# Attention scores from two fp32r parts of q and k in half of the array's rows, in a new order of TensorE's work

## The chip, the cores and the metric

The kernel runs on one core of one Trainium2 chip. The metric is the device time of one execution, in microseconds (us); the kernel before takes 1211.42 us, the median of three runs (1211.42, 1213.09, 1211.42).

## The reference, cut to what matters

One layer of a vision transformer on 8 images of 512 tokens of 256 features. Only the first part is touched, self-attention with 16 heads of 16 features:

```python
qkv = jnp.einsum('bysd,ed->byse', x, w_qkv) + b_qkv
qkv = qkv.reshape(B, S, NUM_HEADS, 3 * HEAD_DIM).transpose(0, 2, 1, 3)
q, k, v = jnp.split(qkv, 3, axis=-1)
logits = jnp.einsum('bhqd,bhkd->bhqk', q, k) / math.sqrt(HEAD_DIM)
attn = jax.nn.softmax(logits, axis=-1)
vals = jnp.einsum('bhqk,bhkd->bhqd', attn, v)
```

After it come the output projection, a state-space layer, and a feed-forward layer with one shared expert and two of eight routed ones. The change leaves them as they are.

## The kernel before

The kernel has four parts: the projections to q, k and v (up to about 108 us of the span), the attention (108 to about 504 us), and then the state-space and shared layers and the routed experts, which fill the rest.

**Projections** (`stage_qkv`). For each of the 8 images ("batch" in the code) TensorE makes four tiles of q and k (`project`, L309, in fp32) and four of v (L318). A score of q and k needs more precision than one bf16 product gives, so each value is cut into three bf16 parts: ScalarE rounds to the high part (L355), VectorE subtracts it (L400), ScalarE rounds the rest to the middle part (L360), VectorE subtracts again (L405). The parts go to DRAM, and are loaded back as rows for the scores. Behind the products of the later images TensorE scores the first two units ahead ("pairs", L286) into `fold_ps`, and VectorE reads their maxima (L413).

**Attention** (`attention_programs`). The work is cut in 32 units: image b times group g of four heads. One unit has 16 tiles by key and 16 tiles by query, 128x512 each. A tile by query (`score_by_query`, L653) serves only to find the maximum of each query's row: VectorE reads two such tiles at once (`take_max`, L746). It is made two units ahead. A tile by key (`score_by_key`, L662) has the keys on the partitions and has the maxima subtracted already, since these stand as more rows of the product; ScalarE takes its exponential straight out of PSUM (L806). The product with the values (`add_pv`, L673) uses the four column strips of the array for the four heads of a group, in fp32. For a product the six pairings of parts stand one under the other, 6 x 16 = 96 rows (99 with the three parts of the maximum).

The way of a maximum: VectorE's result is split in parts by GpSimd (`split_max`, L128 to L135), turned by TensorE (`turn_max`, L685) into a bank of `by_key`, copied out by ScalarE (L799), and put by a DMA from GpSimd's queue into the rows of q (`place_max`, L140). The next unit's first tile by key waits for that (`max_in`).

**What sets the order.** It is written out by hand. Each engine runs its own list, and semaphores join them. In `tensor.unit` the loop over j = 0 to 15 issues tile j by key, then as many tiles by query as `QUERIES[j % 4]` says, and at some j the products with the values (`LATE_PV`, `EARLY_PV`), the turn of the maxima (`MAX_BEHIND`) and the turn of the finished heads (`TURN_HEADS`). The tiles by key go round three banks of PSUM (`KEY_BANKS = 3`): a tile, or a turn of maxima, waits until ScalarE has read what was put three jobs earlier (`key_bank_free`). The tiles by query have four banks, two pairs. The last two units have no tiles by query; there `beside` puts work of the next stage between the tiles by key.

## Time and profile before

| | |
|---|---|
| median of three runs | 1211.42 us |
| the profiled execution | 1215.23 us, its span 1213.4 us |
| TensorE busy | 1156.5 us, 95% |
| VectorE busy | 785.6 us, 65% |
| ScalarE busy | 504.9 us, 42% |
| granted TensorE clock, mean | 0.988 |

### The profile page before, as it was taken

The numbers are of one execution on the slowest core, as the hardware profiler recorded it, in microseconds if no ns is written. First come the engines' busy times: TensorE is split into PE (matmuls) and PEld (weight loads), VectorE is DVE, ScalarE is ACT, GpSimd is POOL, SyncE is SP. The second block draws the span as 40 slices with busy tenths as digits, with TensorE's granted clock in tenths as the row PEclk, the third lists the DMA queues.
The fourth block names the chain that finished last, engine by engine and source line by source line (L and its number), as shares of the span: only waits on it lengthen the run. The fifth ranks groups of instructions, "written<-read, shape, count | busy, mean of one in ns | idle before, by whom it ended". The sixth has DMA issues, their size and how long they took to land.

```text
span 1213.4 us, 20444 instructions
## 1 busy us (share of the span) xinstructions
PE 1156.5 (95%) x5606; PEld 693.2 (57%) x5607; DVE 785.6 (65%) x1404; ACT 504.9 (42%) x890; POOL 395.7 (33%) x515
## 2 busy tenths in 40 slices
PE   6998999999999999989999999987999999999996
PEld 3654333333333334556655666556888888888885
DVE  3688888888888887687887677774333333333332
ACT  3444777777777777522122121421222221222221
POOL 3002621010101010223334433263554445554443
PEclk9998999999999999999999999998999999999999
DMA  8885333232323332124225541222333333333332
GB/s 304 254 263 173 88 86 88 84 105 68 103 71 100 88 84 63 55 103 105 48 57 105 104 87 40 66 36 53 50 48 51 52 53 52 50 49 50 51 53 35
DMA packets 108685, 105.32 MB, mean 87 GB/s; under 512 B 42464, under 2 KB 97904, under 8 KB 108624
## 3 DMA queue, kind: packets, MB, share of 16 engines
q1 hardware_dynamic: 90528, 81.18, 24.2%
q0 software_dynamic: 18112, 23.57, 11.4%
q8 instruction: 24, 0.39, 0.1%
q14 instruction: 21, 0.17, 0.1%
HBM read 64.88 MB, written 39.68 MB: 86 GB/s over the span
## 4 chain that ended last, share of the span: by engine, by line
PE 64%; issue 15%; POOL 5%; DVE 4%; DMA 2%; ACT 1%; SPq 0%; POOLq 0%; DVEq 0%; ACTq 0%
PE mix_pairs L73 17%; PE pv L673 10%; PE mix_made L1730 10%; PE by_key L662 10%; PE by_query L653 8%; PE mix_turn L1723 3%; PE mix_made L1198 2%; DVE k_mix_u L1404 2%; POOL mix_h L1067 2%; POOL mix_h L1064 1%; PE mix_turn L1703 1%; POOL kept_table L1083 1%; PE by_query L694 1%; POOL mix_rstd L1054 1%; DVE mix_stats L1394 1%
## 5 line engine op out<-in xcount | busy, mean ns | idle before, releaser
L746 DVE TENSOR_REDUCE k_neg_max<-by_query 128x2 f32<-128x1024 f32 x240 | 282.6, 1219 | 55.8 <-PE by_query L653 55.1
L806 ACT ACTIVATE k_wu_e<-by_key 128x512 f32<-128x512 f32 x512 | 278.4, 600 | 84.9 <-PE by_key L662 81.5
L662 PE MATMUL by_key<-k_wg_e 99*128 99x512 bf16 x512 | 180.4, 385 | 3.1 <-DVE pv L782 3.0
L1682 POOL DMA_INDIRECT out_rows<-x_y,k_slot x72 | 114.0, 1583 | 178.2 <-DVE x_y L1811 160.5
L1772 ACT ACTIVATE x_gate<-mix_pairs 128x512 f32<-128x512 f32 x72 | 43.0, 597 | 305.9 <-PE mix_pairs L73 305.9
L653 PE MATMUL by_query<-k_wg_e 96*128 96x512 bf16 x480 | 145.1, 383 | 0.3
L1730 PE MATMUL mix_made<-k_wd_e,x_acts_T 128*128 x576 | 136.0, 379 | 0.8 <-ACT x_acts_T L1781 0.8
L673 PE MATMUL pv<-k_wu_e,k_wd_e 128*17 128x512 f32 x1024 | 134.5, 598 | 0.2 <-ACT k_wu_e L806 0.2
L73 PE MATMUL mix_pairs<-w_short,x_T 128*128 x288 | 134.2, 466 | 0.0
L662 PEld LDWEIGHTS by_key<-k_wg_e 99*128 99x128 bf16 x512 | 42.4, 97 | 144.3 <-ACT k_wu_e L806 81.0
L1730 PEld LDWEIGHTS mix_made<-k_wd_e,x_acts_T 128*128 128x128 f32 x576 | 108.8, 189 | 18.8 <-issue 1.0
L73 PE MATMUL mix_pairs<-w_short,x_rest 128*128 x288 | 114.0, 396 | 0.0
L1795 DVE CAST x_T<-mix_turn 128x256 fp32r<-128x256 f32 x72 | 30.6, 424 | 106.2 <-PE mix_turn L1703 104.7
L128 POOL CAST k_max_parts<-k_neg_max 128x16 bf16<-128x16 f32 x32 | 6.4, 201 | 251.7 <-PE by_key L662 231.0
L1811 DVE TENSOR_SCALAR x_y<-mix_made,k_slot 128x256 f32<-128x256 f32 x72 | 34.8, 483 | 78.0 <-DMA out_rows<-x_y,k_slot 56.7
L915 POOL DMA_INDIRECT k_x_in<-kept_x_rows,k_slot x72 | 72.9, 1013 | 27.2 <-issue 21.6
L653 PEld LDWEIGHTS by_query<-k_wg_e 96*128 96x128 bf16 x480 | 45.0, 99 | 61.4 <-DVE k_wd_e L760 13.3
L1804 DVE TENSOR_TENSOR x_acts<-x_gate,mix_pairs 128x512 f32<-128x512 f32 x72 | 49.5, 687 | 46.4 <-PE mix_pairs L73 46.4
L1083 POOL DMA_INDIRECT kept_table<-k_pay,k_slot_i x64 | 64.6, 1009 | 22.3 <-issue 18.4
L309 PE MATMUL qk_ps<-k_wu_e,k_wqkv 128*128 128x512 f32 x128 | 60.1, 612 | 9.5 <-DMA k_wu_e<-in_xT 9.5
L1241 PE MATMUL mix_pairs<-k_mix_u_T,k_wg_s 128*128 128x512 f32 x128 | 64.4, 627 | 4.5 <-DVE mix_act_T L1376 4.5
L73 PEld LDWEIGHTS mix_pairs<-w_short,x_rest 128*128 128x128 f32 x288 | 54.5, 189 | 13.5
(220 smaller groups left out, 1722.6 us busy)
## 6 DMA issues: line engine op xcount, KB each, us to landing
k_wg_e<-kept_qk SPq DMA_DIRECT2D x384, 64.0 KB, 2.1
kept_qk<-k_qk_parts SPq DMA_DIRECT2D x32, 384.0 KB, 2.9
kept_v<-k_v_ones SPq DMA_DIRECT2D x8, 544.0 KB, 5.1
k_wd_e<-kept_v SPq DMA_DIRECT2D x32, 136.0 KB, 2.6
k_wu_e<-in_xT POOLq DMA_DIRECT2D x8, 512.0 KB, 5.8
kept_heads<-k_wd_e SPq DMA_DIRECT2D x8, 512.0 KB, 2.9
k_heads_in<-kept_heads SPq DMA_DIRECT2D x8, 512.0 KB
k_wg_e<-in_wg_e SPq DMA_DIRECT2D x8, 512.0 KB, 4.6
```

The lines of the kernel that those rows point to most:

```text
L73: mm = pe.matmul(out, short(lhs[a]), short(rhs[b]), start=(start and n == 0), stop=(stop and n == 2))
L309: mm = pe.matmul(qk_ps[:, j, :], wqkv[:, c, j * P:(j + 1) * P], xt[:, par, c, :], start=(c == 0), stop=(c == DC - 1))
L653: pe.matmul(by_query[:, pair_bank(b, g, k // 2) + k % 2, :], q_rows[0:KROWS, g, h, t * P:(t + 1) * P], k_rows[0:KROWS, g, h, :], start=Tru ...
L662: pe.matmul(by_key[:, key_bank(job), :], k_rows[0:SROWS, g, h, kt * P:(kt + 1) * P], q_rows[0:SROWS, g, h, :], start=True, stop=True).then ...
L673: mm = pe.matmul(pv[PV_ROWS * h:PV_ROWS * h + VW, :], v_unit[:, g, kt, h, :], probs[:, G * (kt // 2) + h, kt % 2, :], start=(kt == 0), sto ...
L746: dve.tensor_reduce(neg_max[:, g % 2, 2 * n:2 * n + 2], by_query[:, bank:bank + 2, :], AX.X, ALU.max, negate=True).then_inc(query_read, 1)
L806: act.activation(probs[:, key_tile(j) // 2 * G + j // 2 % G, j % 2, :], by_key[:, key_bank(job), :], ACT.Exp, scale=float(HD) ** -0.5).the ...
L915: pool.indirect_dma_start(out=mem["x_in"][:, r % FIRST_X, :], out_offset=None, in_=dram["x_rows"], in_offset=bass.IndirectOffsetOnAxis(ap= ...
L1083: pool.indirect_dma_start(out=dram["table"], in_offset=None, in_=mem["pay"][:, 1 - par, t, n, :], out_offset=bass.IndirectOffsetOnAxis(ap= ...
L1241: mm = pe.matmul(pairs[:, m % 2, n, :], w[:, c, m * P:(m + 1) * P], u2_T[:, c, :], start=(c == 0), stop=(c == DC - 1))
L1682: pool.indirect_dma_start(out=dram["out"], in_=y[:, r % 2, :], in_offset=None, compute_op=ALU.add, out_offset=bass.IndirectOffsetOnAxis(ap ...
L1730: mm = pe.matmul(ps_y[:, r % 2, 0:D], acts_T[:, m, :], mem["wd_e"][:, bass.ds(e, 1), m, :], start=(m == 0), stop=(m == FC - 1))
```

## The change

q and k are cut in two parts instead of three, in fp32r (fp32 data that TensorE multiplies in one pass), so there are three pairings, 3 x 16 = 48 rows, and 50 with the maximum's two parts. These fit half of the partitions. `rows_of(g)` puts groups 0 and 3 into partitions 0 to 63, and 1 and 2 into 64 to 127; the tiles by key of unit g and those by query of unit g + 2 thus always lie in different halves. The tiles in the projections pair group 0 with group 1. ScalarE's middle part and VectorE's low part go away. The parts in DRAM hold 8 bytes a value instead of 6; a unit is loaded by 6 DMAs of twice the size instead of 12. In the projections the scores ahead move into the last four images, and the turn of the first maxima to the end of the last image; the loads of the first units move from images 1, 3, 5, 6 to 1, 2, 5, 6. In a unit, the order of TensorE's work, the place of the turns and of ScalarE's copies change.

```diff
-PARTS = 3
-Q_PART = (0, 0, 0, 1, 1, 2)
-K_PART = (0, 1, 2, 0, 1, 0)
+PARTS = 2
+Q_PART = (0, 0, 1)
+K_PART = (0, 1, 0)
...
-MAX_BEHIND = 3
-HEADS_BEHIND = 5
+MAX_BEHIND = 8
+HEADS_BEHIND = 4
...
+def rows_of(g, count=HALF, first=0):
+    half = HALF * ((g + 1) // 2 % 2)
+    return slice(half + first, half + count)
...
     pool.sem_inc(step)
-    pool.tensor_copy(mem["max_parts"][:, 0, :], rows).then_inc(done, 1)
+    pool.tensor_copy(short(mem["max_parts"][:, 0, :]), rows).then_inc(done, 1)
     pool.wait_ge(done, base + 1)
-    pool.tensor_tensor(mem["neg_rest"][:, :], rows, mem["max_parts"][:, 0, :], ALU.subtract).then_inc(done, 1)
-    pool.wait_ge(done, base + 2)
-    pool.sem_inc(step)
-    pool.tensor_copy(mem["max_parts"][:, 1, :], mem["neg_rest"][:, :]).then_inc(done, 1)
-    pool.wait_ge(done, base + 3)
-    pool.tensor_tensor(mem["max_parts"][:, 2, :], mem["neg_rest"][:, :], mem["max_parts"][:, 1, :],
-                       ALU.subtract).then_inc(done, 1)
+    pool.tensor_tensor(short(mem["max_parts"][:, 1, :]), rows, mem["max_parts"][:, 0, :], ALU.subtract).then_inc(done, 1)
...
-        PAIR_BATCH = B - 5
-        TURN_BATCH, TURN_BEHIND = B - 2, 1
+        PAIR_BATCH = B - 4
+        PAIR_BEHIND = {b: (("qk", 0), ("qk", 2), ("v", 0), ("v", 2)) for b in range(PAIR_BATCH, B - 1)}
...
+                h, t = pair // TT, pair % TT
+                for g in range(2):
+                    rows = rows_of(g, KROWS)
+                    mm = pe.matmul(fold_ps[:, g, :], short(q_rows[rows, 0, h, t * P:(t + 1) * P]),
+                                   short(k_rows[rows, 0, h, :]), start=True, stop=True)
...
+                if isinstance(b, int) and b == B - 1:
+                    turn_first_max()
...
-            def middle_part(b, j):
-                act.wait_ge(qk_out[j], b + 1)
-                act.activation(qk_parts[:, j, 1, :], qk_rest[:, j, :], ACT.Copy).then_inc(middle_made, 1)
...
-            def low_part(b, j):
-                dve.wait_ge(middle_made, 4 * b + j + 1)
-                dve.tensor_tensor(qk_parts[:, j, 2, :], qk_rest[:, j, :], qk_parts[:, j, 1, :],
-                                  ALU.subtract).then_inc(cut[j], 1)
...
-    LATE_PV = {3: 2, 7: 3}
-    EARLY_PV = {11: 0, 15: 1}
-
-    QUERIES = (0, 2, 2, 0)
-    TURN_HEADS = 12
+    LATE_PV = {2: 2, 6: 3}
+    EARLY_PV = {10: 0, 14: 1}
+
+    QUERIES = (1, 1, 0, 2)
+    TURN_HEADS = 10
+
+    COPY_PV = 8
...
             pe.matmul(by_query[:, pair_bank(b, g, k // 2) + k % 2, :],
-                      q_rows[0:KROWS, g, h, t * P:(t + 1) * P], k_rows[0:KROWS, g, h, :],
+                      short(q_rows[rows_of(g, KROWS), g // 2, h, t * P:(t + 1) * P]), short(k_rows[rows_of(g, KROWS), g // 2, h, :]),
...
-            pe.matmul(by_key[:, key_bank(job), :], k_rows[0:SROWS, g, h, kt * P:(kt + 1) * P],
-                      q_rows[0:SROWS, g, h, :], start=True, stop=True).then_inc(key_filled, 1)
+            pe.matmul(by_key[:, key_bank(job), :], short(k_rows[rows_of(g, SROWS), g // 2, h, kt * P:(kt + 1) * P]),
+                      short(q_rows[rows_of(g, SROWS), g // 2, h, :]), start=True, stop=True).then_inc(key_filled, 1)
...
             for j in range(G * TT):
                 score_by_key(b, g, j)
+                if j == MAX_BEHIND and next_max:
+                    turn_max(b1, g1)
+                if j == TURN_HEADS and prev:
+                    turn_heads(bp, gp)
                 for _ in range(QUERIES[j % 4]):
...
-                if j == 7 and not (isinstance(b, int) and b == 0 and g == 0):
+                if j == COPY_PV and not (isinstance(b, int) and b == 0 and g == 0):
```

TensorE in the middle of a unit before, from a product with the values (`pv`) to the next; the rows L661 are register work of the sequencer:

```order
L673 MATMUL pv<-k_wu_e,k_wd_e 17x512 x4
L661 REGISTER_ALU
L662 MATMUL by_key<-k_wg_e 128x512
L661 REGISTER_ALU
L662 MATMUL by_key<-k_wg_e 128x512
L653 MATMUL by_query<-k_wg_e 128x512 x2
L661 REGISTER_ALU
L662 MATMUL by_key<-k_wg_e 128x512
L652 REGISTER_ALU
L653 MATMUL by_query<-k_wg_e 128x512 x2
L661 REGISTER_ALU
L662 MATMUL by_key<-k_wg_e 128x512
```

There were four tiles by key and four by query between two products with the values, the tiles by query two by two. The same place in the changed kernel (`by_key` is now L643, `by_query` L634, `pv` L654):

```order
L654 MATMUL pv<-k_wu_e,k_wd_e 17x512 x4
L642 REGISTER_ALU
L643 MATMUL by_key<-q_rows,k_rows 128x512
L633 REGISTER_ALU
L634 MATMUL by_query<-k_rows,q_rows 128x512 x2
L642 REGISTER_ALU
L643 MATMUL by_key<-q_rows,k_rows 128x512
L634 MATMUL by_query<-k_rows,q_rows 128x512
L642 REGISTER_ALU
L643 MATMUL by_key<-q_rows,k_rows 128x512
L634 MATMUL by_query<-k_rows,q_rows 128x512
L642 REGISTER_ALU
```

A fourth tile by key ends the piece, and the next product with the values stands right behind it: still four and four, but they alternate, and the fourth tile by key is the last thing before the values. The one piece of a unit that holds both turns, in the changed kernel, right behind tile 8 by key (L666 turns the maxima, L675 the heads):

```order
L666 MATMUL by_key<-k_ident,k_wd_e 128x128
L633 REGISTER_ALU
L634 MATMUL by_query<-k_rows,q_rows 128x512
L642 REGISTER_ALU
L643 MATMUL by_key<-q_rows,k_rows 128x512
L634 MATMUL by_query<-k_rows,q_rows 128x512
L642 REGISTER_ALU
L643 MATMUL by_key<-q_rows,k_rows 128x512
L672 REGISTER_ALU
L675 MATMUL by_query<-k_ident,heads_T 128x128 x4
L654 MATMUL pv<-k_wu_e,k_wd_e 17x512 x4
```

Before, the turn of the maxima (L685) stood behind tile 3 and the turn of the heads (L694) behind tile 12. ScalarE's list at the same place (L787 is the exponential, L780 the copy of the turned maxima, L799 that of the finished heads out of `pv`):

```order
L787 ACTIVATE k_wu_e<-by_key 128x512
L777 REGISTER_ALU
L780 ACTIVATE k_wd_e<-by_key 32x128
L797 REGISTER_ALU
L798 REGISTER_ALU
L799 ACTIVATE heads_T<-pv 128x512
L786 REGISTER_ALU
```

Both copies now stand behind exponential 8; before, they stood behind exponentials 3 and 7.

## Rows read from the trace of the kernel before

**Rows 1.** Busy time, 60 us of attention: span, PE, PEld, DVE, ACT, POOL, clock, DMA.

```profile
240.00:300.00 60.00, 59.53 (x343) 18.54 (x341) 49.24 (x51) 46.23 (x90) 7.23 (x25) 1.00 0.31 87
```

**Rows 2.** Turns of the maxima, one a unit: ns min/median/max, first and last start.

```profile
L685 PE MATMUL by_key<-k_identb,k_max_parts x31: 219/227/314, 110.5 to 476.1; 128*128 128x128 bf16 x31
```

**Rows 3.** Timeline of TensorE in one unit: start, duration, engine, line, count.

```profile
302.43 0.38 PE L662 MATMUL by_key<-k_wg_e 99*128 99x512 bf16 x1
302.75 1.05 PE L673 MATMUL pv<-k_wu_e,k_wd_e 128*17 128x512 f32 x8
303.73 0.60 PE L662 MATMUL by_key<-k_wg_e 99*128 99x512 bf16 x2
304.17 0.60 PE L653 MATMUL by_query<-k_wg_e 96*128 96x512 bf16 x2
...
305.87 1.05 PE L673 MATMUL pv<-k_wu_e,k_wd_e 128*17 128x512 f32 x8
...
308.69 1.05 PE L673 MATMUL pv<-k_wu_e,k_wd_e 128*17 128x512 f32 x8
```

**Rows 4.** Timeline, the turn of the heads in a unit.

```profile
300.58 0.60 PE L694 MATMUL by_query<-k_ident,heads_T 128*128 128x128 f32 x4
301.02 0.38 PE L662 MATMUL by_key<-k_wg_e 99*128 99x512 bf16 x1
```

**Rows 5.** Timeline of TensorE in the projections, and where the attention begins.

```profile
48.08 0.60 PE L286 MATMUL fold_ps<-k_wg_e 96*128 96x512 bf16 x2
48.51 3.60 PE L309 MATMUL qk_ps<-k_wu_e,k_wqkv 128*128 128x512 f32 x8
...
103.31 1.89 PE L318 MATMUL v_ps<-k_wqkv,k_wu_e 128*128 128x256 f32 x8
108.17 0.61 PE L662 MATMUL by_key<-k_wg_e 99*128 99x512 bf16 x2 [2.97 <-DVE pv L782]
```

**Rows 6.** Timeline of the experts: fp32r matmuls and their weight loads (PEld).

```profile
1000.99 0.19 PEld L73 LDWEIGHTS mix_pairs<-w_short,x_T 128*128 128x128 f32 x1
1001.02 0.48 PE L73 MATMUL mix_pairs<-w_short,x_T 128*128 x1
1001.10 0.19 PEld L73 LDWEIGHTS mix_pairs<-wu_rest,x_T 128*128 128x128 f32 x1
1001.33 0.40 PE L73 MATMUL mix_pairs<-wu_rest,x_T 128*128 x1
```

**Rows 7.** Groups by line, whole span: busy, mean ns of one, idle before.

```profile
L662 PEld LDWEIGHTS by_key<-k_wg_e 99*128 99x128 bf16 x512 | 42.4, 97 | 144.3 <-ACT k_wu_e L806 81.0 <-ACT k_max_rows L799 25.5 <-issue 8.1
L405 DVE TENSOR_TENSOR k_qk_parts<-k_wu_e,k_qk_parts 128x512 bf16<-128x512 f32 x32 | 21.8, 682 | 0.3
```

**Rows 8.** Timeline of VectorE: two readings of maxima; normalising between two.

```profile
121.95 2.36 DVE L746 TENSOR_REDUCE k_neg_max<-by_query 128x2 f32<-128x1024 f32 x2 [0.47 <-PE by_query L653]
...
301.22 0.26 DVE L756 RECIPROCAL row_sum<-by_query 128x16 f32<-128x16 f32 x1 [0.26 <-PE by_query L694]
...
301.87 1.22 DVE L746 TENSOR_REDUCE k_neg_max<-by_query 128x2 f32<-128x1024 f32 x1
```

**Rows 9.** Timeline, ScalarE and GpSimd behind the tiles by key.

```profile
304.16 1.57 ACT L806 ACTIVATE k_wu_e<-by_key 128x512 f32<-128x512 f32 x3 [0.71 <-PE by_key L662]
306.17 0.26 ACT L799 ACTIVATE k_max_rows<-by_key 48x128 bf16<-48x128 bf16 x1
307.12 0.62 POOL L140 DMA_DIRECT2D k_wg_e<-k_max_rows  x1 [1.54 <-ACT k_max_rows L799]
```

**Rows 10.** Timelines of the first unit: TensorE waits there for a bank.

```profile
110.70 0.60 ACT L806 ACTIVATE k_wu_e<-by_key 128x512 f32<-128x512 f32 x1 [0.53 <-PE by_key L662]
...
111.35 0.61 PE L662 MATMUL by_key<-k_wg_e 99*128 99x512 bf16 x1 [0.16 <-ACT k_wu_e L806]
```

**Rows 11.** DMA issues of the page: count, size each, median us to landing.

```profile
kept_qk<-k_qk_parts SPq DMA_DIRECT2D x32, 384.0 KB, 2.9
```

**Rows 12.** Line L140: the DMA of the maxima, all 32.

```profile
DMA to landing us min/median/max: 2.1/2.7/5.1
```

More of the change, by code:

```diff
@@ L166, in stage_qkv @@
         x_used = [sem(f"x_used{n}") for n in range(2)]
-        qk_out = [sem(f"qk_out{n}") for n in range(4)]
         cut = [sem(f"cut{n}") for n in range(4)]
@@ L220, in _ @@
             pool.wait_ge(ones_set, 2)
-            pool.memset(mem["k_rows"][KROWS:SROWS, :, :, :], 1.0).then_inc(ones_set, 1)
+            for half in range(2):
+                pool.memset(mem["k_rows"][HALF * half + HALF // 2:HALF * (half + 1), :, :, :], 1.0).then_inc(ones_set, 1)
             with pool.Fori(1, B // 2) as i:
@@ L256, in store @@
                         sp.wait_ge(parts_stored[j], 16)
-                        for n in range(ROW_LOADS // 4 * j, ROW_LOADS // 4 * (j + 1)):
+                        for n in LOAD_BEHIND[j]:
                             load_rows(sp, mem, dram, 0, unit, n)
@@ L266, in _ @@
             store(0)
+            sp.wait_ge(ones_set, 4)
             for b in range(1, B):
@@ L281, in score_pair @@
                     pe.wait_ge(pair_read, pair)
-                if pair == FIRST_PAIR[TURN_BATCH]:
-                    pe.wait_ge(first_copied, 1)
-                for k in (2 * n, 2 * n + 1):
-                    h, t = k // TT, k % TT
-                    mm = pe.matmul(fold_ps[:, k % 2, :], q_rows[0:KROWS, g, h, t * P:(t + 1) * P],
-                                   k_rows[0:KROWS, g, h, :], start=True, stop=True)
+                h, t = pair // TT, pair % TT
+                for g in range(2):
+                    rows = rows_of(g, KROWS)
+                    mm = pe.matmul(fold_ps[:, g, :], short(q_rows[rows, 0, h, t * P:(t + 1) * P]),
+                                   short(k_rows[rows, 0, h, :]), start=True, stop=True)
                 mm.then_inc(pair_scored, 1)
@@ L417, in cut_and_add @@
                 b = 2 * i + par
-                rest(b, 0)
-                take_pairs_behind(b, "rest", 0)
-                for j in range(1, 4):
+                for j in range(4):
                     rest(b, j)
                     take_pairs_behind(b, "rest", j)
-                    low_part(b, j - 1)
-                    take_pairs_behind(b, "low", j - 1)
-                low_part(b, 3)
                 dve.wait_ge(v_stored, 16 * b)
@@ L523, in turned_max @@
     def turned_max(bank):
-        return by_key[:, bank, 0:P // 2].bitcast(BF16)
+        return by_key[:, bank, 0:P]
     PAIRS = G * TT // 2
@@ L1930, in program @@
             mem["w_short"] = later.enter_context(nc.sbuf_tensor("w_short", [P, E, 2, DC, F], FP32))
+        with ExitStack() as early:
+            for name in ("q_rows", "k_rows"):
+                mem[name] = early.enter_context(nc.sbuf_tensor(name, [P, NG // 2, G, S], FP32))
         until_cut = ctx.enter_context(ExitStack())
```

103 lines of the change are left out of this document (43 added, 60 removed).

## The prediction, made before the changed kernel was run

> **What bounds the kernel now.** I read the busy time by stretches first. In 60 us of attention TensorE is busy for 59.5 us at a granted clock of 1.00, that is at 2.4 GHz; VectorE has 49 us, ScalarE 46 and the DMA 31% [rows 1]. So TensorE's list is the time there, and the question is how long one unit of it is. The turn of the maxima comes once a unit: 30 units between 110.5 and 476.1 us, 12.19 us each [rows 2]. The timeline shows what they are made of [rows 3]. Between two products with the values lie four tiles by key and four by query; from one product to the next it is 2.82 us (305.87 to 308.69), and 3.12 with the turn of the maxima in it (302.75 to 305.87), which so costs 0.30. In such a piece a tile follows a tile by 0.22 (303.73 to 304.17 is two), the last tile and the values stand 0.32 apart, and the values hold the array for 0.98 (302.75 to 303.73). The turn of the heads takes 0.44 [rows 4]. In the projections TensorE runs from product to product as well [rows 5].
>
> **The unit in the new kernel.** TensorE's own work first. An fp32r tile of 512 columns follows another by 0.23 to 0.24 in the experts (1001.10, when the weights of one are in and the load of the next begins, to 1001.33) [rows 6]. A tile that has to begin with its weight load has 0.11 more in front of it (1000.99 to 1001.10), and its result is there 0.40 after that [rows 6]. For bf16 the load's record is 97 ns [rows 7] against 190 here. If a tile by key and one by query, in the two halves, stream together, a piece is: load 0.11, three steps of 0.235 to the last pair (0.82), 0.32 to the values, 0.98: 2.12 us. No row shows two matmuls in two halves of the rows, so the price of a pair lies between 0.235 and 0.47 (one behind the other). The nearest row is the product with the values: its eight instructions in four column strips take 0.98 us [rows 3], where eight of L309 of the same 512 columns take 3.4 to 3.6 [rows 5]. Strips of the array do work at once here, so I take 0.235.
>
> By TensorE's work alone a unit would be 4 x 2.12 + 0.30 + 0.54 = 9.3 us (0.54: heads and one more change of mode), and VectorE would set it: eight readings 1.14 apart and 0.65 for normalising [rows 8], 9.8 us. I don't believe in either, because of the three banks of the tiles by key. The new order issues keys 3, 0, 1, 2 and then the values. Key 2 needs the bank of key 3, so it waits for ScalarE's exponential of the first tile of its own piece. Step by step, from the weight load of key 3: result at 0.51 (0.11 + 0.40), exponential from 0.55 (the row has 0.43 from a tile's start to the exponential's, 303.73 to 304.16, with a result at 0.38 [rows 3, 9]), end at 1.15 (0.60), bank free at 1.20: the row of the first unit has exactly this wait, exponential 110.70 + 0.60, tile at 111.35 [rows 10]. Then key 2's load 0.11, to the values 0.32, values 0.98: a piece is 2.61 us. Any price of a pair up to 0.40 is hidden in it. ScalarE's own need, four exponentials 0.49 apart [rows 9], is 1.9, and VectorE's 2.3; neither holds it.
>
> The piece with both turns. Key 8 streams at 0.35, and its exponential follows that of key 7 by 0.49: 1.04 to 1.64. ScalarE then copies the maxima (0.26, from 1.53) and the heads (0.60 as every 128x512 out of PSUM, from 1.68), till 2.28, since both copies now stand behind exponential 8. TensorE has done key 10 by then (load at 1.69, bank of key 8) and waits: turn of the heads at 2.33, 0.44, change of mode 0.10, values at 2.87, end 3.85. The unit is 3 x 2.61 + 3.85 = 11.68 us. Against 12.19 it is 0.51 less, times 30 units: **15.3 us gained**. Its bounds: 11.2 if ScalarE takes both copies sooner or a half of the array delivers sooner, 12.3 if each change between half, whole and strips costs another 0.1 (six a unit).
>
> A rule speaks against the change at this place. The row shows 0.32 instead of 0.22 between the last tile and the values [rows 3], a loss of 0.10 when the way of using the array changes. The Trainium skill (TensorEngine Tiling (Array Packing), Key Properties) says that changing the tiling mode, not just the tile, drains the engine; the trace agrees with 0.10 us. By it the turn of the maxima, a whole-array matmul between half-array tiles, costs two more drains. They are hidden in the waits above, but not where TensorE has no waits: in the projections and in the last two units. With the rule these cost the 3.5 us reckoned next, without it about nothing.
>
> **The other parts.**
> - Pairs in the projections: 16, now 0.43 each (48.08 to 48.51) [rows 5]. New: change 0.10, load 0.11, tiles 0.235, and again about 0.05 to get back: 0.50, so 16 x 0.07 = +1. Bounds: -3 (both tiles 0.235, no change) to +4 (tiles one behind the other, 0.68).
> - VectorE loses 32 subtractions, 21.8 us [rows 7], and ScalarE as many roundings. Both lie beside TensorE's products, which run on: worth 0.
> - Stores of q and k grow from 384 to 512 KB; one lands in 2.9 us [rows 11], so about 1 us later each. A tile's next store is a whole image later, 10 us and more: 0, at most +3 if a unit's loads and the stores of images 1 and 2 meet.
> - Start of the attention: the first turn of maxima now comes after the last product of the projections, and the first tile by key waits for it. From that product's end: turn 0.23, copy 0.31, GpSimd 0.69 (306.43 to 307.12 [rows 9]), landing 2.7 [rows 12]: 3.9 us, against 3.0 now (105.20 to 108.17) [rows 5]. Landing may take the 5.1 of the slowest [rows 12]: +0.9 to +3.3, I take +1.5.
> - The last two units have no tile by query. 32 tiles by key are 0.015 longer, and about 14 whole-array pieces stand between them, each with a drain of 0.10 and an open load of 0.11: 3.4; part of that lies in waits for ScalarE. I take +2.5, bounds 0 and +5.
> - The maxima's way in a unit: turned behind key 8 at 0.67, copied till 1.79, issued by GpSimd at 2.48, landed at 5.2; the next unit's first tile comes at 3.85 + 2.61 + 0.24 = 6.7. Hidden, with 1.5 us left. Splitting has two steps instead of four, and more time: 0.
> - The unit's loads: the same bytes, 7 issues for 13, at a DMA share of 0.31 [rows 1]: 0. Behind 504 us nothing changes.
>
> Sum: -15.3 + 1 + 1.5 + 2.5 = -10.3 us. The profiled execution, 1215.23 us with a span of 1213.4, would be 1204.9; it stands 3.8 above the median of the runs. Against that median, 1211.42, I predict **1201 us**.
>
> **Rivals.**
> 1. The halves don't work at once. For: the nearest row has strips of columns, not halves of rows; two weight loads of 0.19 have to go into one step. Against: the values' row, and a load really holds its place for 0.11 only. Price: key 2 streams at 0.11 + 7 x 0.235 = 1.76, piece 3.06; the piece with the turns 4.07; unit 13.25, +1.06 x 30 = 32, pairs in the projections +4, the rest +4: **1251 us**, slower. It decides from a step of 0.40 on: then key 2 is late by itself, and at a piece of 2.74 the gain is gone. The Trainium skill (the same page and section) says that tiles can load weights and multiply in parallel; no row here shows it for halves. By that rule this rival falls.
> 2. The bank doesn't hold, because it comes free before the exponential's record ends or because TensorE's records are longer than its results take. Then VectorE sets the unit, 9.8 to 10.4 with the joins: 2.1 x 30 = 63 gained, less 5: **1153 us**. Against it stand rows 10.
> 3. The changes of mode cost twice what the row has, everywhere: unit 12.0 (0.19 x 30 = 6 gained), the ends 8 instead of 5: **1213 us**, no change.
>
> **How the numbers follow.** Forecast 0.72, rival 1 0.14, rival 2 0.08, rival 3 0.06. The forecast alone goes from 1188 to 1214 (unit 11.2 to 12.0, the ends 1 to 9). The range that leaves out rival 1 and most of rival 2 is 1178 to 1222. A measurement tells 0.2%, 2.4 us, from no change. Faster: 0.93 of the forecast and rival 2, 0.75. Within: 0.03 of the forecast and half of rival 3, 0.06. Slower: 0.02, 0.14 and 0.03, 0.19.
>
> **What would show it.** Turns of the maxima 11.7 us apart. In the timeline of TensorE a tile by key and one by query with starts a few hundredths apart, then the fourth key of a piece released by ScalarE, and the turn of the heads by ScalarE's copy. Values to values 2.6 us three times and 3.9 once. VectorE idle for about 2 us a unit. The first tile by key 4 to 5 us behind the projections' last product. Wrong would be: key and query 0.2 us apart all the way (rival 1), TensorE waiting mainly for VectorE's readings (rival 2), or a first tile of each unit that waits for the DMA of the maxima.

## The result and the profile after

The changed kernel takes 1219.84 us (median of 4, 1219.16 to 1220.78), the kernel before 1211.42 on the same chip. The ratio is 1.0067, 95% interval 1.0049 to 1.0084: slower by 0.7%, where 1201 us and faster were forecast. The unit of the attention did become about as short as forecast. What was gained there, and more, went at the two ends of the attention, in the projections and, in part, to the clock.

The busy times by stretches, in the same 60 us as [rows 1]:

```profile
240.00:300.00 60.00, 58.92 (x358) 22.79 (x350) 51.16 (x52) 45.13 (x92) 5.10 (x15) 1.00 0.60 90
```

Columns as in [rows 1]: TensorE's records cover nearly all the time (58.92 us, before 59.53), but now two of them often run at once, one in each half of the rows. The turns of the maxima, which answer to [rows 2]:

```profile
L666 PE MATMUL by_key<-k_ident,k_wd_e x31: 327/328/472, 119.7 to 481.9; 128*128 128x128 f32 x31
```

Thirty intervals take 362.3 us, 12.08 each instead of 12.19. The mean hides several cases. The steady units take 11.69 to 11.73 three times and about 11.94 each fourth time; the first two take 15.24 and 12.19, the last one 17.37. Forecast were 11.68. TensorE's timeline around the join of two images, with ScalarE's rows below it, answers to [rows 3, 4, 9]:

```profile
300.86 0.49 PE L643 MATMUL by_key<-q_rows,k_rows 50*128 50x512 f32 x1
301.55 0.65 PE L675 MATMUL by_query<-k_ident,heads_T 128*128 128x128 f32 x4 [0.20 <-ACT heads_T L799]
302.13 1.05 PE L654 MATMUL pv<-k_wu_e,k_wd_e 128*17 128x512 f32 x8
303.11 0.50 PE L643 MATMUL by_key<-q_rows,k_rows 50*128 50x512 f32 x1
303.12 0.50 PE L634 MATMUL by_query<-k_rows,q_rows 48*128 48x512 f32 x1
...
303.69 0.39 PE L643 MATMUL by_key<-q_rows,k_rows 50*128 50x512 f32 x1
...
304.30 0.49 PE L643 MATMUL by_key<-q_rows,k_rows 50*128 50x512 f32 x1
304.72 1.05 PE L654 MATMUL pv<-k_wu_e,k_wd_e 128*17 128x512 f32 x8
305.71 0.50 PE L643 MATMUL by_key<-q_rows,k_rows 50*128 50x512 f32 x1
305.71 0.50 PE L634 MATMUL by_query<-k_rows,q_rows 48*128 48x512 f32 x1
306.05 0.39 PE L643 MATMUL by_key<-q_rows,k_rows 50*128 50x512 f32 x1
...
306.89 0.50 PE L643 MATMUL by_key<-q_rows,k_rows 50*128 50x512 f32 x1
```

```profile
303.65 2.06 ACT L787 ACTIVATE k_wu_e<-by_key 128x512 f32<-128x512 f32 x4 [1.27 <-PE by_key L643]
306.24 2.27 ACT L787 ACTIVATE k_wu_e<-by_key 128x512 f32<-128x512 f32 x4 [0.53 <-PE by_key L643]
```

A tile by key and one by query start 0.01 us apart or together (303.11 and 303.12, both 305.71): the halves work at once. From 302.13 to 304.72, product with the values to product with the values, is the ordinary piece, 2.59 us for the 2.61 forecast. Its fourth key starts at 304.30, 0.61 behind the third, when ScalarE's exponential of the first (from 303.65, about 0.60) has given the bank back. That is the chain the prediction built on [rows 10]. The piece behind it is another case: here the next image begins behind the first key, and the third key of the piece needs the bank of that first one, only two jobs old. So it waits for the exponential (from 306.24, about 0.60), to 306.89 instead of about 306.28. This piece takes 2.83 and comes once in four units. The turn of the heads at 301.55 waits for ScalarE's copy, also as forecast.

By the profiled executions' own spans, 1213.4 before and 1218.6 after, the time went here:

| stretch | before | after | measured | forecast |
|---|---|---|---|---|
| to the end of the projections' last product [rows 5] | 105.20 | 108.85 | +3.65 | +1 |
| from there to the first key | 2.97 | 5.66 | +2.7 | +1.5 |
| first key to that of unit 30 (30 units) | 365.97 | 356.2 | -9.8 | -15.3 |
| from there to the last turn of heads | 30.2 | 37.1 | +6.9 | +2.5 |
| all behind it | 709.1 | 710.8 | +1.7 | 0 |

The sum is +5.2, where -10.3 was forecast. In the third line 5.5 us are missing. The 27 units between the third turn of the maxima and the thirtieth take 317.5 us, 11.76 each for 11.68; that is 2.1 of it. The other 3.4 lie in the first units, where TensorE's clock is low. The clock over their time (windows of 6 us; the last columns are granted clock, DMA share, GB/s), in the changed kernel:

```profile
114.00:120.00 6.00, 5.49 (x18) 3.24 (x18) 4.25 (x5) 4.32 (x9) 0.00 (x0) 0.50 0.00 0
120.00:126.00 6.00, 6.00 (x25) 2.42 (x28) 3.91 (x4) 3.73 (x8) 3.53 (x16) 0.50 0.02 6
126.00:132.00 6.00, 6.00 (x28) 2.14 (x22) 3.04 (x3) 2.17 (x4) 3.39 (x17) 0.50 0.53 88
132.00:138.00 6.00, 5.88 (x37) 2.49 (x33) 5.29 (x6) 4.73 (x10) 1.10 (x4) 0.94 0.47 68
```

and before, around its first key at 108.17 (windows of 3 us):

```profile
108.00:111.00 3.00, 2.83 (x10) 1.06 (x10) 1.87 (x3) 1.87 (x4) 0.00 (x0) 0.72 0.29 118
111.00:114.00 3.00, 2.84 (x8) 0.98 (x8) 1.75 (x2) 2.13 (x5) 1.46 (x6) 0.50 0.04 4
114.00:117.00 3.00, 3.00 (x10) 0.97 (x8) 2.04 (x3) 2.06 (x4) 2.14 (x12) 0.64 0.03 8
117.00:120.00 3.00, 3.00 (x21) 0.95 (x24) 2.50 (x3) 2.24 (x6) 2.14 (x12) 1.00 0.00 0
```

After the gap both kernels run at the lower level, 0.50 or 1.2 GHz. The kernel before is back at 2.4 GHz from about 116 us, the changed one in this execution only from about 132.

Two of these figures differ from execution to execution. In the runs below that leave TensorE's list in the projections alone, their last product ends between 108.4 and 110.1 us. And the part behind the last turn of heads, which no run touches, takes 706.5 to 712.8: the +1.7 in the last line lies within that, and totals of single executions a few us apart can't be told from each other. The readings inside a unit repeat to a few hundredths.

### The profile page after: what moved, and what is told of

It is laid out like the page before. It is cut to its first block, busy times and chain, and to the rows that moved or that the text cites. A ratio compares the mean times of both kernels' runs of the same rounds, so it can differ in the third digit from the quotient of the medians.

```text
span 1218.6 us, 19832 instructions
## 1 busy us (share of the span) xinstructions
PE 1154.1 (95%) x5606; PEld 716.6 (59%) x5607; DVE 765.6 (63%) x1372; ACT 475.2 (39%) x858; POOL 380.9 (31%) x452
## 4 chain that ended last, share of the span: by engine, by line
PE 60%; issue 14%; POOL 4%; DMA 4%; DVE 3%; ACT 3%; SPq 1%; POOLq 0%; ACTq 0%; DVEq 0%
PE mix_pairs L74 16%; PE by_key L643 11%; PE pv L654 10%; PE mix_made L1711 9%; PE by_query L634 3%; DMA out_rows<-mix_h 3%; PE mix_turn L1704 2%; PE by_query L675 2%; DVE k_mix_u L1385 2%; POOL mix_h L1048 1%; PE mix_pairs L1222 1%; POOL mix_h L1045 1%; PE mix_turn L1684 1%; POOL mix_rstd L1035 1%; ACT heads_T L799 1%
## 5 line engine op out<-in xcount | busy, mean ns | idle before, releaser
L787 ACT ACTIVATE k_wu_e<-by_key 128x512 f32<-128x512 f32 x512 | 268.7, 598 | 110.8 <-PE by_key L643 109.7
L643 PE MATMUL by_key<-q_rows,k_rows 50*128 50x512 f32 x512 | 206.2, 467 | 6.7 <-DVE pv L763 5.5
L643 PEld LDWEIGHTS by_key<-q_rows,k_rows 50*128 50x128 f32 x512 | 87.4, 189 | 164.1 <-ACT k_wu_e L787 147.6
L634 PE MATMUL by_query<-k_rows,q_rows 48*128 48x512 f32 x480 | 165.0, 450 | 0.8 <-DVE k_neg_max L727 0.8
L654 PE MATMUL pv<-k_wu_e,k_wd_e 128*17 128x512 f32 x1024 | 137.1, 608 | 0.7 <-ACT k_wu_e L787 0.7
L634 PEld LDWEIGHTS by_query<-k_rows,q_rows 48*128 48x128 f32 x480 | 78.2, 190 | 18.6 <-DVE k_neg_max L727 11.9
L143 POOL DMA_DIRECT2D q_rows<-k_wd_e x32 | 19.8, 618 | 162.7 <-ACT k_wd_e L780 154.8
L1222 PE MATMUL mix_pairs<-k_mix_u_T,k_wu_s 128*128 128x512 f32 x128 | 62.4, 611 | 0.0
```

The source lines that it names most:

```text
L634: pe.matmul(by_query[:, pair_bank(b, g, k // 2) + k % 2, :], short(q_rows[rows_of(g, KROWS), g // 2, h, t * P:(t + 1) * P]), short(k_rows[ ...
L643: pe.matmul(by_key[:, key_bank(job), :], short(k_rows[rows_of(g, SROWS), g // 2, h, kt * P:(kt + 1) * P]), short(q_rows[rows_of(g, SROWS), ...
L654: mm = pe.matmul(pv[PV_ROWS * h:PV_ROWS * h + VW, :], v_unit[:, g, kt, h, :], probs[:, G * (kt // 2) + h, kt % 2, :], start=(kt == 0), sto ...
L787: act.activation(probs[:, key_tile(j) // 2 * G + j // 2 % G, j % 2, :], by_key[:, key_bank(job), :], ACT.Exp, scale=float(HD) ** -0.5).the ...
L1222: mm = pe.matmul(pairs[:, m % 2, n, :], w[:, c, m * P:(m + 1) * P], u2_T[:, c, :], start=(c == 0), stop=(c == DC - 1))
```

## Experiments

Ratios are to the kernel before, run on the same chip alongside. "After" is the changed kernel. Every edit is made on it.

**The halves.** Both tiles of a pair in the same half of the rows:

```diff
-    half = HALF * ((g + 1) // 2 % 2)
+    half = HALF * (g % 2)
```

> Groups 0 and 2 in partitions 0 to 63, 1 and 3 in 64 to 127, so that the tiles by key and by query that alternate lie in the same half; the pairs in the projections still lie in two halves. Theory A (the two halves work at once, and this is what makes the unit short): tiles 0.235 us one behind the other, a piece 3.06 us, a unit about 13.2 us, in all about 45 us more than the changed kernel, 1265. Rival (the gain per unit comes only from the order and the turns): a unit stays at 11.7 to 12.

Measured: 1255.01 us, one execution, units 12.85 and 13.30. Key and query now follow each other by 0.24:

```profile
302.71 0.39 PE L643 MATMUL by_key<-q_rows,k_rows 50*128 50x512 f32 x1
302.95 0.39 PE L634 MATMUL by_query<-k_rows,q_rows 48*128 48x512 f32 x1
303.19 0.49 PE L643 MATMUL by_key<-q_rows,k_rows 50*128 50x512 f32 x1
```

The pieces of a unit are 3.04, 3.04, 4.16 and 2.60; the formula of rival 1 gave 3.06 and, with the turns, 4.07. The one of 2.60 joins two units, which still lie in different halves; hence 12.85 and not the 13.2 expected. So the two halves together are worth at least 1.15 us a unit, 35 us in all, and rival 1 is out: it is what would have happened without them. (The Trainium skill, TensorEngine Tiling (Array Packing), Key Properties, says that tiles load weights and multiply in parallel; the rows of the changed kernel, both tiles at 305.71, agree.)

**The bank.** Exponentials of images 1 to 6 over 384 of 512 columns, so that ScalarE gives a bank back sooner and TensorE's and VectorE's work stays as it is (the kernel leaves out the last quarter of these exponentials):

```diff
+            cols = S if isinstance(b, int) else 384
-            act.activation(probs[..., j % 2, :], by_key[:, key_bank(job), :], ACT.Exp,
+            act.activation(probs[..., j % 2, 0:cols], by_key[:, key_bank(job), 0:cols], ACT.Exp,
```

> From image 1 to the last but one each exponential takes 384 of its 512 columns (the last quarter of the weights keeps old values, so that part of the computation is left out). Nothing else changes. Theory A (the fourth key of a piece waits for the bank, so the chain weight load, tile, exponential, tile sets the piece): the exponential takes about 0.12 less and so does each of the three pieces without turns (2.48 instead of 2.59), with the piece of the turns a unit is 0.5 to 0.7 shorter, 11.1 instead of 11.70, span about 15 less. Theory B (TensorE's own work sets the piece, the wait for ScalarE is only what the record shows last): the unit stays 11.6 to 11.7. Theory C (VectorE's readings of 1.17 set it): also unchanged, and VectorE would have no idle time in a unit.

Measured: steady units 11.15 to 11.18 (before the edit 11.69 to 11.73), 1207.05 us in one execution. A piece is 2.49, from key at 302.52 to key at 305.01:

```profile
302.52 0.50 PE L643 MATMUL by_key<-q_rows,k_rows 50*128 50x512 f32 x1
...
304.03 1.05 PE L654 MATMUL pv<-k_wu_e,k_wd_e 128*17 128x512 f32 x8
305.01 0.49 PE L643 MATMUL by_key<-q_rows,k_rows 50*128 50x512 f32 x1
```

TensorE and VectorE did the same work as before and the unit became 0.53 shorter: the chain through the bank sets it. (ScalarE's four exponentials of a piece are recorded over 2.06 of its 2.59 us, so it is the way through the bank and not ScalarE's sum of work.)

**The turn of the heads.** ScalarE copies the heads ahead of the maxima (`copy_pv` before `copy_max` in `scalar`'s `unit`).

> ScalarE copies the finished heads before the turned maxima instead of after them. Theory A (the turn of the heads waits for ScalarE's copy, which stands behind exponential 8 and the copy of maxima): the piece with both turns is 0.15 us shorter, a unit 11.55 instead of 11.70, 4 us less in all. Theory B (something else holds that piece, such as the drains): a unit stays at 11.70, or gets longer because the maxima land later.

Measured: 1215.2 us, ratio 1.002 (1.0008 to 1.0033), unit 11.59. The edit takes 0.12 a unit, 3.5 us in all, which the prediction's bound of "ScalarE takes both copies sooner" had in it. By the two ratios the gain would be 5.7 us; their intervals allow for either.

**The clock.** First five whole-array fp32 matmuls of 512 columns in the gap ahead of the attention:

```diff
                     turn_first_max()
+                    for _ in range(FILL):   # 5
+                        pe.matmul(fold_ps[:, 1, :], wqkv[:, 0, 0:P], xt[:, par, 0, :], start=True, stop=True)
```

> Five fp32 matmuls of 512 columns, whose result nobody reads, are put behind the first turn of maxima, into TensorE's gap before the attention. Theory A (the changed kernel is slow at the start of attention because TensorE's clock is at its lower level for 18 us after the gap): granted clock 1.00 all through 114 to 132 us, the first two turns of maxima about 12 us apart instead of 15.2, and 5 to 6 us less than the changed kernel, about 1214. Theory B (the first units are slow for another reason, such as GpSimd's powers or the first loads): the intervals stay at 15 us, the time within 1 us of the changed kernel's.

Measured: 1218.0 us, ratio 1.0036 (1.0023 to 1.005), where about 1214 was expected; the first two intervals are 13.32 and 12.19. The clock was 1.00 when the attention began and fell about 118.5 us, with TensorE at work in unit 0. So filling the gap was not enough. The next two runs keep this filler and add 16 matmuls of 128 columns at two places of unit 0, alike but for the rows:

```diff
+                if j in LATE_PV and not prev:
+                    for n in range(16):
+                        pe.matmul(pv[PV_ROWS * (n % G):PV_ROWS * (n % G) + VW, P * (n // G):P * (n // G) + P],
+                                  ident[0:P, 0:VW], ident[0:P, :], start=True, stop=True)   # or rows 0:HALF
```

> Is it the half arrays that let the clock fall in the first unit? Five fp32 matmuls of 512 columns in the gap ahead of the attention, as in the filler run before, and in unit 0, at the two places where the products with the values are still missing, 16 fp32 matmuls of 128 columns over all 128 rows (they write strips that the first product of unit 0 overwrites; the results stay the same). Theory A (tiles in half arrays alone don't hold the clock, whole-array work between them does): granted clock 1.00 or near it from 114 to 126 us, where the filler alone had 0.90 and 0.53; second interval of the turns 11.6 to 11.8 instead of 12.19, the first 12.5 to 13.3; span 1215 to 1217. Theory B (the fall is the late answer to the gap ahead of the attention, whatever runs in unit 0): clock 0.50 to 0.60 for 120 to 126 us as with the filler alone, span 1217 to 1218. Theory C (TensorE's waits in unit 0 do it, and any work that fills them holds the clock): as A here, and as A in the run with 64 rows.

> The same with the 16 matmuls at each of the two places of unit 0 over rows 0 to 63 alone, so as many instructions and columns, in half of the array. Theory A (whole-array work between the half-array tiles holds the clock): clock 0.50 to 0.60 in 120 to 126 us, as with the filler alone. Theory B (late answer to the gap): the same 0.50 to 0.60. Theory C (filling TensorE's waits is enough): near 1.00 from 114 to 126. The pair of runs tells the three apart: A has only the run with 128 rows at 1.00, B has neither, C both.

With 128 rows:

```profile
114.00:117.00 3.00, 2.00 (x39) 1.38 (x40) 1.69 (x2) 1.47 (x3) 0.00 (x0) 1.00 0.00 0
117.00:120.00 3.00, 3.00 (x44) 1.83 (x44) 2.37 (x3) 2.17 (x5) 0.00 (x0) 1.00 0.00 0
120.00:123.00 3.00, 3.00 (x19) 1.22 (x19) 2.37 (x3) 2.27 (x5) 0.89 (x3) 1.00 0.03 8
123.00:126.00 3.00, 3.00 (x22) 1.33 (x19) 2.43 (x3) 2.38 (x5) 2.14 (x12) 1.00 0.03 6
```

With 64 rows:

```profile
114.00:117.00 3.00, 2.59 (x41) 1.77 (x43) 1.58 (x2) 1.57 (x3) 0.00 (x0) 0.86 0.00 0
117.00:120.00 3.00, 3.00 (x36) 2.07 (x36) 2.34 (x2) 2.08 (x4) 0.00 (x0) 0.50 0.00 0
120.00:123.00 3.00, 3.00 (x21) 1.40 (x13) 1.24 (x2) 1.37 (x4) 0.00 (x0) 0.50 0.01 3
123.00:126.00 3.00, 3.00 (x14) 0.99 (x14) 1.22 (x1) 1.13 (x3) 2.17 (x9) 0.50 0.06 11
```

Only the rows differ, and only the run over the whole array keeps 2.4 GHz. That is what theory A says: up to tile 10 by key unit 0 has no products with the values, half-array tiles are nearly all its work, and behind the filler the clock fell during them. Each of the two is one execution, but the other runs with a filler side with them: the two at the end of this section, with whole-array work in unit 0, stay at 1.00, and the filler alone fell. First intervals of the turns: 11.40 and 11.82 against 12.13 and 12.19. The spans are the same, 1216.8 and 1216.9. The last turn of the maxima came 2.5 us sooner with 128 rows; what lies behind it took 2.4 longer, within the differences that this part shows from execution to execution.

What brings the clock back is open, and the price of its fall is not fixed. Unit 0 was the same in all runs without a filler but the same-half run. From the first key to the third turn of the maxima it is 32.6 us in the changed kernel and in the bank run and 32.7 in the copy run, with 20 us at 0.50; 30.5 in the first run on the last two units, with 14; and 29.4 to 29.5 in four others (the 128 rows in the projections, both of the start, the whole-array keys), with only 10. None of those four was meant to touch the clock. With it at 1.00 throughout it is 28.3 to 28.4. The short case, in the run with the first transfer behind the barrier:

```profile
120.00:126.00 6.00, 6.00 (x31) 2.12 (x30) 4.13 (x4) 3.29 (x8) 3.87 (x18) 0.74 0.03 6
```

So of the 3.4 us lost in the first units about 3.1 were absent in four other executions, with no edit against them; whole-array work in unit 0 is worth 1.1 us against these and 4.2 against the profiled one.

**The projections' pairs.** Over all 128 rows, the spare rows of q zero (the products of both groups are added, so the first maxima are others than the computation wants):

```diff
+                pool.memset(mem["q_rows"][HALF * half + HALF // 2:HALF * (half + 1), :, :, :], 0.0).then_inc(ones_set, 1)
-                    rows = rows_of(g, KROWS)
+                    rows = slice(0, P)
```

> The 16 pairs of tiles in the projections over all 128 rows instead of one half each (the spare rows of q are zero; the products of both halves are added, so the maxima of the first two units are others, and only that part of the computation changes). Theory A (what makes a pair cost 0.63 instead of 0.43 is the change from whole to half array and back, 0.20 and 0.19 as in the last two units): no such change is left, the two tiles stream one behind the other at 0.235 each, a pair costs 0.47 to 0.50 and the end of the projections' last product comes at 106.0 to 107.2 instead of 108.85. Theory B (the change between fp32 and fp32r operands, or a weight load that begins only when the product before it is out, costs it, whatever the rows): the second tile adds 0.235 to 0.63, a pair costs 0.85, and the last product ends at 112 to 113.

The rows of TensorE in the last image, after:

```profile
99.96 1.98 PE L306 MATMUL qk_ps<-k_wu_e,k_wqkv 128*128 128x512 f32 x4
101.87 0.49 PE L284 MATMUL fold_ps<-k_rows,q_rows 48*128 48x512 f32 x2
102.30 1.98 PE L306 MATMUL qk_ps<-k_wu_e,k_wqkv 128*128 128x512 f32 x4
104.70 0.51 PE L284 MATMUL fold_ps<-k_rows,q_rows 48*128 48x512 f32 x2 [0.42 <-DVE k_neg_max L396]
```

and with 128 rows:

```profile
98.17 1.88 PE L307 MATMUL qk_ps<-k_wu_e,k_wqkv 128*128 128x512 f32 x4
99.77 0.74 PE L285 MATMUL fold_ps<-k_rows,q_rows 128*128 128x512 f32 x2
100.35 1.88 PE L307 MATMUL qk_ps<-k_wu_e,k_wqkv 128*128 128x512 f32 x4
```

A pair with its four products takes 2.34 after (99.96 to 102.30) and 2.18 here (98.17 to 100.35), although here its tiles run one behind the other. Less four products of 0.43, a pair is 0.62 in halves and 0.46 over the whole array. The last product ends at 107.0 instead of 108.85, below all other runs (108.4 to 110.1). Whole arrays one after the other beat half arrays at once where the neighbours are whole: going to halves and back costs about 0.38 (0.62 less 0.235), more than the second tile of 0.235.

**The start of the attention.** GpSimd's transfer of the first maxima as the first thing behind the barrier (`place_max(pool, mem, 0)` moved from the projections to the start of `gpsimd`), and in another run the first turn behind the third value tile:

```diff
                     score_pairs_behind(b, "v", t)
-                if isinstance(b, int) and b == B - 1:
-                    turn_first_max()
+                    if isinstance(b, int) and b == B - 1 and t == 2:
+                        turn_first_max()
```

> GpSimd's transfer of the first maxima is issued as the first thing of the attention instead of the last thing of the projections. In the changed kernel it is issued at 110.07, the split of unit 1 is done at 111.25, and all engines enter the attention only at about 113.8. Theory A (the barrier between the two parts waits till GpSimd's own transfer has landed): without it all engines enter at 111.4 to 111.8, VectorE sets its bank to zero at 111.6 to 112 instead of 113.97, and the first tile by key comes at 114.2 to 115 (issue, 2.7 of landing), so about where it was. Theory B (the barrier waits for something else, as the stores of the values by SyncE's queue): VectorE's memset stays at 113.8 to 114.1, the issue comes behind it, and the first tile by key at 116.5 to 117.5.

> The first turn of the maxima behind the third of the four value tiles of the last image instead of behind the last. Theory A (the barrier into the attention waits till GpSimd's transfer of the maxima has landed, so the chain turn, copy, issue, landing sets the start): everything behind the turn comes 1.8 us sooner, VectorE's memset at about 112.0 to 112.6 instead of 113.97, the first tile by key at 112.4 to 113.0 instead of 114.51, unless the store of the values (issued at about 110.2) holds the barrier at 111.3 to 111.8 or so. Theory B (the barrier waits for something else): memset stays at 113.8 to 114.1 and the first tile by key with it.

After, where GpSimd issues (110.07) and VectorE enters the attention (113.97):

```profile
110.07 0.66 POOL L143 DMA_DIRECT2D q_rows<-k_wd_e  x1 [2.42 <-ACT k_wd_e L360]
```

```profile
113.97 0.48 DVE L763 MEMSET pv<- 128x512 f32 x1 [4.33 <-PEq L150]
```

With the transfer moved behind the barrier:

```profile
111.27 0.48 DVE L760 MEMSET pv<- 128x512 f32 x1 [1.15 <-PEq L150]
111.74 0.66 POOL L143 DMA_DIRECT2D q_rows<-k_wd_e  x1 [1.64 <-POOLq L150]
...
114.09 0.76 PE L640 MATMUL by_key<-q_rows,k_rows 50*128 50x512 f32 x1 [4.66 <-DMA q_rows<-k_wd_e]
```

The barrier came 2.7 us sooner (3.2, counted from the last pair of the projections, which was 0.5 later here), so it had waited for GpSimd's transfer. The first key gains little, 0.4, since now it waits for the landing itself. With the earlier turn GpSimd issued at 109.78, VectorE's memset came at 112.87 and the first key at 113.41, 1.1 sooner, where 1.8 was expected. But in that execution the last pair stood at 105.29 for 104.70, 0.6 late. Counted from it, the issue is 0.9 sooner (the turn had to wait for GpSimd's split of the maxima, 107.75 to 108.25) and the memset 1.7; the rest, 0.8, is the way from issue to memset, 3.9 after and 3.1 here, with a landing of 3.1 and 2.2. Both runs, 1216.86 and 1218.0 us, are single ones.

**The last two units.** First the whole-array pieces brought together directly behind the products with the values, so that fewer changes of mode are left:

```diff
-        PROJECT_BEHIND, STATE_BEHIND = (4, 5, 6, 8), (8, 9, 10, 12)
+        PROJECT_BEHIND, STATE_BEHIND = (6, 6, 10, 10), (10, 10, 14, 14)
```

> In the last two units the pieces of the next stage between tiles by key are moved right behind products with the values, so that TensorE goes into and out of half-array use some ten times less; the same work otherwise. Theory A (each such visit costs 0.39 us, 0.20 in and 0.19 out): about 4 us less than the changed kernel, about 1216. Theory B (the last units are slow because tiles by key wait for ScalarE's exponentials in the new order): no gain or a loss, since the tiles by key come in denser bursts.

Measured: 1220.21 us, ratio 1.0052 (1.0039 to 1.0065), the two units 1.4 us longer (38.5 for 37.1). Fewer changes, but keys now come four in a row and the last of them waits for its bank, 2.0 us in eight waits, and the turn of the heads waits 0.48. This run could not tell the causes apart. The next does: the keys of the last unit over all 128 rows, with zeros in the other half's rows of q.

```diff
+            if isinstance(b, int) and (b, g) == (LAST, NG - 1):
+                rows = slice(0, P)
+                pe.wait_ge(q_zeroed, h + 1)
...
+                        dve.wait_ge(key_filled, key_jobs_to(b, key_job(b, g - 1, G * TT // 2 + 2 * h + 1)))
+                        dve.memset(q_rows[HALF:P, g // 2, h, :], 0.0).then_inc(q_zeroed, 1)
```

> The sixteen tiles by key of the very last unit run over all 128 rows instead of rows 0 to 50: the spare rows of q are zero, and VectorE sets the other unit's rows of q to zero as soon as they are no longer read (four memsets of 64x512 in time in which it is idle), so the results stay the same. From the first key of that unit to the turn of its heads the changed kernel has about 11 places where half-array tiles and whole-array work follow each other. Theory A (each change from half to whole array costs 0.20 and back 0.19): the products stand nearer by 0.2 on either side of a key, the last unit is 3 to 4.3 us shorter, span about 1214.5 to 1215.5. Theory B (the cost is that of changing between fp32r and fp32 operands, whatever the rows): nothing changes, span 1218 to 1219. Theory C (the last unit is set by ScalarE's exponentials and VectorE, the changes are hidden in those waits): less than 1 us shorter.

After, then with whole arrays, at the same place:

```profile
495.02 1.13 PE L1196 MATMUL mix_made<-k_mix_u_T,k_m_T 128*128 128x512 f32 x2
496.07 0.50 PE L643 MATMUL by_key<-q_rows,k_rows 50*128 50x512 f32 x1
496.50 1.13 PE L1196 MATMUL mix_made<-k_mix_u_T,k_m_T 128*128 128x512 f32 x2
```

```profile
493.21 1.02 PE L1206 MATMUL mix_made<-k_mix_u_T,k_m_T 128*128 128x512 f32 x2
493.67 0.80 PE L649 MATMUL by_key<-q_rows,k_rows 128*128 128x512 f32 x1
494.31 1.02 PE L1206 MATMUL mix_made<-k_mix_u_T,k_m_T 128*128 128x512 f32 x2
```

And in the kernel before:

```profile
493.80 1.02 PE L1215 MATMUL mix_made<-k_mix_u_T,k_m_T 128*128 128x512 f32 x2
494.66 0.38 PE L662 MATMUL by_key<-k_wg_e 99*128 99x512 bf16 x1
494.88 1.02 PE L1215 MATMUL mix_made<-k_mix_u_T,k_m_T 128*128 128x512 f32 x2
```

One product with its key takes 1.48 after (495.02 to 496.50), 1.10 with whole arrays and 1.08 in the kernel before (493.80 to 494.88). So 0.38 to 0.40 is the price of the half array between whole ones, and the type of the operands has no part in it: with whole arrays they are fp32r between fp32 as well. But from the last turn of the maxima to the last products the run is only 1.5 us shorter (21.71 for 23.20), not 3 to 4.3. I had counted 11 places; at about half of them the neighbour is the product with the values, where nothing changed (two keys take 0.64 to it, 0.66 after), and the first key waited 0.30 for the memset. At six places the neighbour is other work; six times 0.38 less that wait would be 2.0. The time, 1219.19, is one execution, with 712.8 us behind the attention for 710.8.

**All together.** The earlier turn, the filler, whole-array work in unit 0 and the earlier copy of the heads; then the same with the whole-array keys of the last unit:

> All that helped together: the first turn of maxima behind the third value tile of the last image, five fp32 matmuls of 512 columns behind the last value tile, the 16 whole-array matmuls at each of two places of unit 0, and the copy of the heads ahead of that of the maxima. By the parts measured one by one: unit 11.58 instead of 11.73, 29 x 0.13 = 3.8 less (5.1 by its run of five rounds); first tile by key 1.5 to 2 sooner; first interval of the turns 11.3 instead of 15.24 and the second 11.8 instead of 12.19, but unit 0 itself no shorter: 4 less. Sum 9.5 to 11 less than the changed kernel: 1209 to 1211 us, against 1211.4 of before a ratio of 0.998 to 1.000, a difference that can hardly be told. If the gains overlap (a clock that is high in unit 0 at the cost of the fillers, or a lower clock later) it ends at 1212 to 1214.

> The same in the version that joins the filler, the whole-array work in unit 0, the earlier turn and the earlier copy of the heads (1211.33 us, ratio 0.9997 to before). If the change of mode in the last unit is worth what theory A says: 3 to 4.3 less, 1207 to 1208.5 us and a ratio of 0.996 to 0.9975, faster than both kernels. If it is hidden: 1211, no difference from before.

The first: 1211.33 us, ratio 0.9997 (0.9988 to 1.0007). It takes back the whole loss and no more. The second: 1211.3 us, where the kernel before had 1213.8 alongside, ratio 0.9981 (0.997 to 0.9992): 0.2% faster than the kernel before. Against the first that is 1.9 us less, where 3 to 4.3 was expected and the keys alone gave 1.5. Its clock is 1.00 from 108 us to the end of the attention, its steady units take 11.57 and 11.81, its first two 11.40 and 11.77.

## Why the prediction was wrong

The measured 1219.84 us lies above what the forecast allowed itself (1188 to 1214). It is inside 1178 to 1222, but on the other side of the kernel before; of the chance of 0.19 given to slower, 0.14 belonged to rival 1, which did not happen. The mechanism inside the unit was right; the terms around it were not.

- **The unit: right, and 2.1 us short.** 11.68 forecast, 11.70 in three of four units. The mechanism is shown by the bank run, and the same-half run rules rival 1 out. Not seen was the join of two images: an image has 68 bank jobs, which three banks don't divide, so each fourth unit has a key whose bank was used two jobs ago and takes 11.94. That is 0.06 a unit, 1.8 in all.
- **Pairs in the projections: +1 forecast, +3.65 measured.** The failed step is "change 0.10, ... and again about 0.05 to get back". A pair costs 0.62 (2.34 less four products of 0.43), not 0.50, so 16 of them 3.0 more than the 0.43 before; two waits of 0.41 and 0.42 for VectorE's reading come on top, since each image now has four pairs to read. The bound of +4 held it.
- **The start: +1.5 forecast, +2.7 measured.** Turn, copy and GpSimd took 1.22 from the last product's end to the issue, as forecast. Then the transfer landed in 3.1 for 2.7, and the chain did not end there: the engines left the barrier 0.8 later, and VectorE's memset stood another 0.54 ahead of the first key. In the kernel before, that transfer was issued at 87.3 us and had landed long ago.
- **The last two units: +2.5 forecast, +6.9 measured.** The same step failed: each whole-array piece was priced at 0.21, a drain of 0.10 and an open load of 0.11. The 0.10 is from the step of a key to the values [rows 3], which is a change to strips. From half to whole array the step is 0.43 for 0.235, 0.20 more, and the product behind it reaches the next key in 1.05 for the 0.86 before, 0.19 more. The Trainium skill (TensorEngine Tiling (Array Packing), Key Properties) says the change of mode drains the engine; the runs agree, with 0.38 to 0.40 for both ways against the 0.21 that the prediction took. The two units have ten changes into other whole-array work and eleven out of it, at this price about 4 us (an estimate; the run with whole-array keys took back 1.5 of it in one of the units). What is left was not tried apart: 0.22 and 0.44 of new waits, 0.69 for 0.25 ahead of the last products, and 0.43 for 0.31 from a single key to the values.
- **The clock: 0 forecast, about 3.4 lost in the profiled execution.** No step of the prediction spoke of it: it reads [rows 1] at 1.00, and not the stretch behind the gap, where the kernel before also fell to 0.50. The pair of runs with 128 and 64 rows shows that the clock held with whole-array work in unit 0 and fell without it; four other executions lost only about 0.3 there against the forecast, and why is open.
- **Behind 504 us: 0 forecast, +1.7.** This is within the 706.5 to 712.8 that the same instructions take in the other runs, and no reading against the forecast.

The largest single miss is the last two units, 4.4 us, then the clock, 3.4; pairs 2.65, the unit 2.1, the part behind 1.7, the start 1.2. The forecast's own range (1188 to 1214) held the ends between 1 and 9. They came to 13.3 without the clock's part, 3.65, 2.7 and 6.9: each term was small and each was too low, two of them by the same figure for the change of mode. Rival 3 had named this figure, but put most of its price into the unit, where the bank hides it, and only 3 us more into the ends.

## What to carry to other kernels

A gain inside the loop is measured in the loop; what a new way of using the array costs is paid at the ends, where no wait hides it, so price each change of mode from a row of that very change. Read the granted clock of the stretch behind a gap too, and ask what kind of work will stand there after the change; here whole-array work held the clock and half-array work did not. Before a few us are explained, see how much the untouched parts differ between executions. Four tiles in a row over three banks make the reader's latency the time, however fast the tiles are.

## What the runs showed of the hardware

- Two fp32r tiles in the two halves of the rows start 0.00 to 0.01 us apart and follow by 0.235 as a pair; in one half they stand 0.24 apart each.
- Half-array matmuls did not hold the clock in unit 0: at the same count of instructions and columns 1.00 with 128 rows, a fall to 0.50 with 64. How long it then stays at 0.50 differed between executions of the same unit, 10 to 20 us. In the steady units, where products with the values over all 128 rows stand between the pairs, it stays at 1.00.
- A visit of a half-array tile between whole-array products costs 0.38 to 0.40 us (1.48 against 1.08 with bf16 keys over 99 rows); with the fp32r key over all 128 rows it is 1.10, so the change of operand type has no part in it.
- The barrier between two parts of the program waited for GpSimd's own transfer to land: 113.97 with it, 111.27 without.
